# A two-layer transformer tower on one core: attention scores in row halves, and the value products one iteration later

## The reference, cut to what matters

```python
def _L0_attn_ref(x, Wq, Wk):              # x: a sequence's normed rows, 512 x 64
    q = jnp.einsum('bnd,ed->bne', x, Wq)
    k = jnp.einsum('bnd,ed->bne', x, Wk)
    attn = jax.nn.softmax(jnp.einsum('bid,bjd->bij', q, k) * scale, axis=-1)
    return jnp.einsum('bij,bjd->bid', attn, x)
def _L1_attn_ref(x, Wq, bq, Wk, bk, Wv, bv, Wo, bo):
    weights = jax.nn.softmax(jnp.einsum('bsd,btd->bst', q, k) * scaling, axis=-1)
    return jnp.einsum('bst,btd->bsd', weights, v) @ Wo.T + bo
```

## Time and profile before

| | |
|---|---|
| median of three runs | 935.1 us (934.78 to 936.87) |
| the profiled execution's own time, and its span | 936.95 us, 935.1 us |
| busy share of the span: PE, PEld, DVE, ACT, POOL | 95%, 68%, 65%, 62%, 41% |
| TensorE's mean granted clock | 0.991 |
| maximum reductions L743 | 256, 170.4 us busy, 687 ns each |
| value products L1058 (records) | 1024, 124.7 us busy |
| score products L1049, L1050, L1024 | 256 each; 113.1, 101.6, 108.2 us busy |
| exponentials L504 | 256, 146.0 us busy, 596 ns each |

### The profile page before, as it was taken

How to read it: one execution, slowest core, us unless ns; L and a number is a source line. 1 busy time by engine, 2 the same in 40 slices (tenths; PEclk the granted TensorE clock), 3 DMA queues, 4 the chain that set the end, 5 groups by cost and what they waited for, 6 DMA issues and landing times.

```text
span 935.1 us, 21847 instructions
## 1 busy us (share of the span) xinstructions
PE 891.6 (95%) x6198; PEld 631.5 (68%) x6198; DVE 603.8 (65%) x2610; ACT 576.6 (62%) x1195; POOL 384.1 (41%) x523
## 2 busy tenths in 40 slices
PE   4879999999999999979999999999999999999998
PEld 2657666666766676656666676666777777777775
DVE  5876777778787899967777777774434343434321
ACT  1336666666666666646666666666666666666664
POOL 0133444444437888834444344443333333333300
PEclk9999999999999999989999999999999999999999
DMA  4000000000001222200000000000000000000000
GB/s 103 2 1 2 1 0 0 0 0 0 1 1 49 72 73 68 75 7 1 1 0 0 0 0 1 1 1 7 12 18 11 17 11 17 11 17 11 18 13 23
DMA packets 18995, 15.13 MB, mean 16 GB/s; under 512 B 5762, under 2 KB 18946, under 8 KB 18946
## 3 DMA queue, kind: packets, MB, share of 16 engines
q1 hardware_dynamic: 18946, 14.52, 5.6%
HBM read 10.32 MB, written 4.19 MB: 16 GB/s over the span
## 4 chain that ended last, share of the span: by engine, by line
PE 83%; DVE 12%; issue 2%; ACT 1%; DMA 1%; DVEq 0%; POOL 0%; SPq 0%; ACTq 0%
PE bank L1226 13%; PE bank L1058 13%; PE bank L1206 7%; PE bank L1024 7%; PE bank L1207 6%; PE bank L971 5%; DVE nmax L743 5%; PE bank L1049 5%; PE bank L1050 5%; PE bank L1135 4%; PE bank L996 3%; PE bank L1037 2%; PE bank L1013 2%; PE bank L1014 2%; PE bank L1003 2%
## 5 line engine op out<-in xcount | busy, mean ns | idle before, releaser
L743 DVE TENSOR_REDUCE nmax<-bank 128x1 fp32r<-128x512 f32 x256 | 170.4, 687 | 47.7 <-PE bank L1024 47.5
L360 POOL TENSOR_TENSOR XS<-XN,XS 128x252 fp32r<-128x252 f32 x128 | 98.0, 765 | 211.6 <-ACT XS L402 211.6
L342 POOL TENSOR_TENSOR rstd<-VE,half 128x4 f32<-128x4 f32 x128 | 129.2, 1009 | 119.6 <-DVE VE L661 119.6
L504 ACT ACTIVATE PT<-bank 128x512 f32<-128x512 f32 x256 | 146.0, 596 | 41.8 <-PE bank L1050 35.5
L354 POOL TENSOR_TENSOR XN<-XC,rstd 128x252 f32<-128x252 f32 x128 | 78.3, 612 | 183.9 <-PE bank L1058 183.7
L556 ACT ACTIVATE PT<-bank 128x512 f32<-128x512 f32 x256 | 132.2, 605 | 3.5 <-PE bank L1207 2.8
L475 ACT ACTIVATE OT<-bank 128x256 f32<-128x256 f32 x96 | 36.8, 384 | 154.3 <-PE bank L1058 103.8
L1058 PE MATMUL bank<-PT,XN 128*64 128x256 f32 x1024 | 124.7, 386 | 0.0
L1226 PE MATMUL bank<-PT,W 128*64 128x256 f32 x1024 | 124.5, 386 | 0.0
L1024 PE MATMUL bank<-X,QH 128*128 128x512 f32 x256 | 108.2, 424 | 8.6 <-DVE nmax L743 1.7
L1049 PE MATMUL bank<-QH,X 128*128 128x512 f32 x256 | 113.1, 442 | 0.5 <-ACT Q L497 0.5
(11 more groups left out here) (136 smaller groups left out, 1506.4 us busy)
## 6 DMA issues: line engine op xcount, KB each, us to landing
WR<-experts SPq DMA_DIRECT2D x64, 129.0 KB, 2.0
out<-H SPq DMA_DIRECT2D x32, 128.0 KB, 1.7
W<-pack SPq DMA_DIRECT2D x5, 252.5 KB, 3.9
W<-pack SPq DMA_DIRECT2D x1, 251.5 KB, 5.1
W<-pack SPq DMA_DIRECT2D x1, 243.0 KB, 5.6
tk<-tokens SPq DMA_DIRECT2D x1, 64.0 KB, 4.4
route_sb<-route SPq DMA_DIRECT2D x1, 0.2 KB
```

The source lines that it names most:

```text
L342: pl.tensor_tensor(rstd[:, par, :], VE[:, par, :], half[:, :], ALU.pow).then_inc(sigma_done, 1)
L504: sc_.activation(PT[:, par, kt, :], bank[4 + kt % 2][:, :], ACT.Exp, scale=SCALE).then_inc(s.e_ready, 1)
L743: v.tensor_reduce(nmax[:, par, t:t + 1], bank[2 + t % 2][:, :], axis=AX, op=ALU.max, negate=True).then_inc(s.max_ready, 1)
```

## The change

It does four things, in both attention stages.

1. **Row halves.** A copy `XD` of the rounded part is put on partitions 64 to 127, beside `X2`'s own on 0 to 63. The score products for the maxima (`pair_for_max`) now use 64 rows each: tile t on the upper half of the rows, tile t+1 on the lower, one right after the other, into banks 2 and 3. The low part of the scores (`low_scores`) is made in the same way into banks 4 and 5. So the maxima no longer see the rest of the keys, and the product of the two rests leaves the scores. The high part (`high_scores`) stays at 128 rows.
2. **Order.** TensorE's body i is now: spread i; project i+1; low part of tiles 0 and 1; turn back i-2; high part of tiles 0 and 1; first pair of maxima of i+1; three of the four values of i-1; second pair of maxima; the fourth; low and high part of tiles 2 and 3; turn i+2.
3. **Another bank for the maxima.** `spread_max` writes bank 0 (row 64, with 65 columns of weights, of which 64 are zero) in place of bank 7. As the turned rows pass through bank 0 too, it waits for `x2_ready` of i+1, which now comes after both copies, `X2` and `XD`. The row goes into row 64 of `QH` in place of row 0 of `Q2`.
4. **ScalarE and VectorE** follow: ScalarE copies bank 6 between exponentials 1 and 2 and rounds after the copies to `X2` and `XD`; VectorE finishes i-2 first, then takes all four maxima of i+1, then its low part.

```diff
@@ -38,7 +38,7 @@
-CONSTS = 7
+CONSTS = 8
@@ -236,8 +236,9 @@
+        XD = sb("XD", [P, 2, SEQ], F32R)
-        nmax = sb("nmax", [P, 2, NT], F32R)
+        nmax = sb("nmax", [P, 2, NT, D + 1], F32R)
@@ -331,8 +332,9 @@
-            pl.memset(f32(XS[:, :, :, D:D + 1]), 0.0).then_inc(consts_set, 1)
+            pl.memset(f32(XS[:, :, :, D:D + 1]), 1.0).then_inc(consts_set, 1)
+            pl.memset(f32(nmax[:, :, :, :]), 0.0).then_inc(consts_set, 1)
@@ -450,7 +452,10 @@
-                sc_.activation(X2[:, par, :], bank[0][:, :], ACT.Copy).then_inc(s.x2_ready, 1)
+                ins = sc_.activation(X2[:, par, :], bank[0][:, :], ACT.Copy)
+                if s is a0 or s is a1:
+                    ins = sc_.activation(XD[D:P, par, :], bank[0][0:D, :], ACT.Copy)
+                ins.then_inc(s.x2_ready, 1)
@@ -490,11 +495,9 @@
                 def body(i, par, lane):
-                    if not known(i) or i >= 1:
-                        evac_o(s, before, bank[6], i - 1, 1 - par)
-                    sc_.activation(Q2[0:1, par, :], bank[7][0:1, :], ACT.Copy).then_inc(s.m_ready, 1)
+                    sc_.activation(QH[D:D + 1, par, :], bank[0][D:D + 1, :], ACT.Copy).then_inc(s.m_ready, 1)
@@ -503,9 +506,10 @@
-                        if kt == 1:
-                            high_on(s, before, after, layer * 2, i + 3, 1 - par, (lane + 3) % 4)
+                        if kt == 1 and (not known(i) or i >= 1):
+                            evac_o(s, before, bank[6], i - 1, 1 - par)
+                    high_on(s, before, after, layer * 2, i + 3, 1 - par, (lane + 3) % 4)
@@ -740,7 +744,7 @@
                 def maxima(i, par, tiles):
                     for t in tiles:
-                        v.tensor_reduce(nmax[:, par, t:t + 1], bank[2 + t % 2][:, :], axis=AX, op=ALU.max,
+                        v.tensor_reduce(nmax[:, par, t, D:D + 1], bank[2 + t % 2][:, :], axis=AX, op=ALU.max,
@@ -753,21 +757,20 @@
+                maxima(0, 0, range(NT))
                 low_parts(0, 0)
-                maxima(0, 0, range(NT))
                 def body(i, par):
+                    if not known(i) or i >= 2:
+                        finish(i - 2, par)
                     if has(i + 1):
+                        maxima(i + 1, 1 - par, range(NT))
                         low_parts(i + 1, 1 - par)
-                        maxima(i + 1, 1 - par, range(2))
-                    if not known(i) or i >= 1:
-                        finish(i - 1, 1 - par)
-                    if has(i + 1):
-                        maxima(i + 1, 1 - par, range(2, NT))
+                finish(NSEQ - 2, 0)
@@ -1013,41 +1016,45 @@
-                def scores_for_max(i, par, t):
+                def pair_for_max(i, par, t):
-                    if t >= 2:
-                        pe.wait_ge(s.max_ready, i * NT + (t - 1))
-                    elif not known(i) or i >= 1:
-                        pe.wait_ge(s.max_ready, i * NT + (t - 1))
-                    mm(bank[2 + t % 2][:, :], QH[:, par, t * P:(t + 1) * P], X2[:, par, :],
-                       start=True, stop=True).then_inc(s.s_ps, 1)
+                    if t == 2 or not known(i) or i >= 1:
+                        pe.wait_ge(s.max_ready, i * NT + t)
+                    for own, rows, keys in ((t, slice(0, D), X2), (t + 1, slice(D, P), XD)):
+                        mm(bank[2 + own % 2][:, :], QH[rows, par, own * P:(own + 1) * P], keys[rows, par, :],
+                           start=True, stop=True).then_inc(s.s_ps, 1)
                 def spread_max(i, par):
+                    if has(i + 1):
+                        pe.wait_ge(s.x2_ready, i + 2)
+                    else:
+                        pe.wait_ge(after.x2_ready, 1)
-                    if not known(i) or i >= 1:
-                        pe.wait_ge(s.m_ready, i)
-                    if not known(i) or i >= 2:
-                        pe.wait_ge(s.h_done, i - 1)
                     for t in range(NT):
-                        last = mm(bank[7][0:1, t * P:(t + 1) * P], nmax[:, par, t:t + 1],
+                        last = mm(bank[0][0:D + 1, t * P:(t + 1) * P], nmax[:, par, t, :],
-                def scores(i, par, kt):
-                    if kt == 0:
-                        pe.wait_ge(s.m_ready, i + 1)
-                    if kt >= 2 or not known(i) or i >= 1:
-                        pe.wait_ge(s.e_ready, i * NT + (kt - 1))
-                    cols = slice(kt * P, (kt + 1) * P)
-                    o = bank[4 + kt % 2][:, :]
-                    mm(o, X2[:, par, cols], QH[:, par, :], start=True, stop=False)
-                    mm(o, X2[:, par, cols], Q2[:, par, :], start=False, stop=True).then_inc(s.st_ps, 1)
+                def low_scores(i, par, kt):
+                    pe.wait_ge(s.ql_ready, i + 1)
+                    if kt == 2 or not known(i) or i >= 1:
+                        pe.wait_ge(s.e_ready, i * NT + kt)
+                    for own, rows, keys in ((kt, slice(0, D), X2), (kt + 1, slice(D, P), XD)):
+                        mm(bank[4 + own % 2][:, :], keys[rows, par, own * P:(own + 1) * P], Q2[rows, par, :],
+                           start=True, stop=False)
+                def high_scores(i, par, kt):
+                    pe.wait_ge(s.m_ready, i + 1)
+                    for own in (kt, kt + 1):
+                        mm(bank[4 + own % 2][:, :], X2[:, par, own * P:(own + 1) * P], QH[:, par, :],
+                           start=False, stop=True).then_inc(s.st_ps, 1)
@@ -1069,34 +1076,36 @@
-                for t in range(NT):
-                    scores_for_max(0, 0, t)
+                for t in (0, 2):
+                    pair_for_max(0, 0, t)
                 def body(i, par, lane):
                     spread_max(i, par)
                     if has(i + 1):
                         project(i + 1, 1 - par)
+                    low_scores(i, par, 0)
+                    if not known(i) or i >= 2:
+                        turn_back(s, before, i - 2, par)
+                    high_scores(i, par, 0)
+                    if has(i + 1):
+                        pair_for_max(i + 1, 1 - par, 0)
+                    if not known(i) or i >= 1:
+                        for kt in range(NT - 1):
+                            values(i - 1, 1 - par, (lane + 3) % 4, kt)
+                    if has(i + 1):
+                        pair_for_max(i + 1, 1 - par, 2)
+                    if not known(i) or i >= 1:
+                        values(i - 1, 1 - par, (lane + 3) % 4, NT - 1)
+                    low_scores(i, par, 2)
+                    high_scores(i, par, 2)
                     turn_on(s, after, i + 2, par)
-                    scores(i, par, 0)
-                    scores(i, par, 1)
-                    if has(i + 1):
-                        scores_for_max(i + 1, 1 - par, 0)
-                    if not known(i) or i >= 1:
-                        turn_back(s, before, i - 1, 1 - par)
-                    scores(i, par, 2)
-                    if has(i + 1):
-                        scores_for_max(i + 1, 1 - par, 1)
-                    scores(i, par, 3)
-                    if has(i + 1):
-                        scores_for_max(i + 1, 1 - par, 2)
-                        scores_for_max(i + 1, 1 - par, 3)
-                    if not has(i + 1):
-                        pe.wait_ge(s.ql_ready, NSEQ)
-                        meanwhile()
-                    for kt in range(NT):
-                        values(i, par, lane, kt)
+                turn_back(s, before, NSEQ - 2, 0)
+                pe.wait_ge(s.ql_ready, NSEQ)
+                meanwhile()
+                for kt in range(NT):
+                    values(NSEQ - 1, 1, (NSEQ - 1) % 4, kt)
@@ -1284,14 +1293,20 @@
     def wide(m):
+    def once(m):
+        m = wide(m)
+        m[:, D] = 0.0
+        return m
     def led(first, m):
-    put("wq0", wide(led(none, x["L0_attn_Wq"])))
+    put("wq0", once(led(none, x["L0_attn_Wq"])))
-    put("wq1", wide(led(x["L1_attn_bq"], x["L1_attn_Wq"])))
+    put("wq1", once(led(x["L1_attn_bq"], x["L1_attn_Wq"])))
@@ -1310,7 +1325,7 @@
-    put("ct", wide(ct))
+    put("ct", once(ct))
```

## The result

The change makes the kernel slower by a fifth: 1120.8 us in the profiled execution, against 935.9 us (median of four runs before); the ratio is 1.198, with a 95% interval of 1.195 to 1.201. Of four runs of the changed kernel two took 1120.8 and 1120.9 us; in the other two (1143 and 1150) the granted clock was lower still, 0.90 in place of 0.92 over the span, and the ratio leaves these out. Forecast were 1035 us and at most 1085: the direction held, the size did not.

What follows compares the result with a forecast made beforehand. The prediction took TensorE to bound the kernel (83% of the chain of waits). 60 intervals x 1.70 = 102 us, less 2, gave +100: span 935.1 to 1035, execution 1037, median forecast 1035 us; range 968 to 1085.

Steps and rivals of the forecast that it cites:

- The new wait: Before the spread into bank 0: TensorE idles some 1.7 us per iteration until `X2` and `XD` are copied.
- The switches: Around row-halved products on TensorE: 0.10 us per switch and 0.11 for first weights, as for column halves.
- The rival of cheap switches: At the row-halved couples: switches cost little, +0.60 us per iteration, 972 us in all; chance 0.18.
- that of halves that run apart: At the couples: halves don't run together, three couples add 0.69 us per iteration, 1076 us; chance 0.10.
- The walk: One attention iteration followed through TensorE, ScalarE and VectorE: from 6.77 to 8.47 us, +1.70; chance as walked 0.46.
- The clock: Rival: granted clock falls after the wait, slowing three value products every second iteration; 40 us more, 1075 us; chance 0.19.
- the sum: Over both attention stages: 60 intervals x 1.70 = 102 us, less 2 for shorter first bodies, +100.
- the long run of values in each iteration: Reason given against the clock falling: TensorE's value products in every iteration; three of them take 1.3 us.
- The range: Whole kernel: 968 to 1085 us, leaving out the faster rival and the meeting of two dear cases.
- the far end where two of the dear cases meet: Whole kernel: two of the slower cases holding at once, left outside the upper bound of 1085 us.
- The rival of a faster kernel: In attention: TensorE stays the bound, copies done by turn's end, maxima hidden; 828 to 925 us, say 880; chance 0.05.

Runs made afterwards that it cites:

- x3: The changed kernel with full 128-row products for the couples, no copy to `XD`, and five idle-time products after each iteration's turn: 1030.9 us.
- x1: The changed kernel with seven idle-time products, read by nobody, after the turn of each iteration: 1067.6 us.
- x6: The kernel before, with values one iteration later in one block, turn of i+2 ahead of them, full rows, maxima in bank 7: 924.0 us, ratio 0.987.
- x8: x6 with idle-time products in the waits at both attention stages' starts and at the ends of the routed stage and a1: 918.2 us, ratio 0.982.

## Why the prediction was wrong, point by point

- **The new wait: right in its place and size, not in all of its reason.** TensorE stands idle for 1.69 us before the spread (forecast: some 1.7), 60 such waits end with the copy to `XD`, and x3 shows that the copy sets the time one for one. But the prediction puts bank 0 first, and by the code the late turn is enough: `project(i + 1)`, right behind the spread, waits for `x2_ready` at i + 2 by itself, the same count. With the maxima in another bank only the spread (0.29 us) could have gone ahead of the wait. That is read from the code; no run has the late turn without bank 0.
- **The switches: right, and for rows too.** Project to low couple 0.33, couple to the next 0.43, a first high product of 0.50: the column-halved rows were the right ones. The rival of cheap switches (972 us) and that of halves that run apart are both refuted. The Trainium skill's page "TensorEngine Tiling (Array Packing)", section "Key Properties", with its drain at a change of mode, agrees with these rows. So does the Trainium skill's page "TensorE: Matmul & The Clock Gate", Part 3, on products of different row groups that start some 4 ns apart (186.79 both).
- **The walk: right in its steps, 0.38 short in its sum** (8.47 forecast, 8.85 measured). Four terms: `X2` to `XD` takes 0.62, not 0.49 (193.38 to 194.00); from the end of `XD` to the spread it is 0.14, not 0.05; the spread with 65 columns of weights holds 0.29, not 0.24; the finish takes 1.13, not 1.00 (187.97 to 189.10). Together 0.40. The last of them is a misread price: the 1.00 of the earlier trace rows is the finish of one iteration, and in 22 of 30 iterations of a0 before it took 1.11 to 1.13. Over 62 intervals the walk at full clock is 24 us dearer; x1, with its first intervals and stage ends, measures 131 us where 100 were forecast.
- **The clock: the step that failed.** In "How the numbers follow" it stood as a rival of the walk, with a chance of 0.19 and its own 40 us, and the sum put it at nothing. It is no rival: x1 shows that TensorE's idle time in the wait, the same wait that makes the walk long, is what brings the clock down; so both come together and add up, 53 us for the clock. The evidence was there, a stretch behind the turn that looked "much the same" as the one before an observed fall; it got a small weight because of "the long run of values in each iteration". That reason did not hold: the fall comes ahead of the values, on project, the low couple, the turn back and the high products (0.54 from 195.01), and the values run at full clock. The rival's 40 us came near by luck. It had 1.3 us in 31 iterations, on the values; measured are 1.33 us (10.11 - 8.78) in 37, on other products.
- **The range** left out "the far end where two of the dear cases meet". That is where the result lies: 1035 + 24 for the walk + 53 for the clock = 1112, above the upper bound of 1085. Of the 9 us that are still missing, 6 lie outside the 62 intervals, between the two attention stages and behind the second, where the clock before was 1.00 (625 to 658) and now is 0.90 (804 to 837).
- **The rival of a faster kernel** failed for the reason that was given against it: the copies stand behind exponentials 2 and 3. x6 shows that its idea was not empty: with the copies beside the values TensorE is the bound again, and the kernel is faster than before.

## What to carry to other kernels

When a producer moves behind the work that used to cover its latency, or a buffer is reused so that one engine waits for another, walk one iteration through all engines before counting what was saved on one of them. Four couples in place of eight full products, 0.92 us less work by count, were worth 0.09 on the chain, and the chain that the wait closes made the iteration 2 us longer. Price a half-array product with its way in and out; alone between full products it costs more than the two full products that it replaces. And ask of idle time on TensorE for two costs, the wait itself and a lower clock after it, and add them where both are at work: idle-time products in a wait tell them apart, and can even stay in.

## What the runs showed of the hardware

- Work added to a waiting TensorE made the kernel faster: 7 products per iteration, 1120.8 to 1067.6 us; in x8, 32 products in the whole kernel, 924.0 to 918.2 us.
- A copy from partitions 0 to 63 of PSUM to partitions 64 to 127 starts 0.62 us after the copy ahead of it from the same bank (193.38 to 194.00), where a rounding starts 0.48 after it (x3: 216.71 to 217.19). Why was not tried.
- Two row-halved products started within 0.01 us of each other in every iteration looked at, and their switches cost what those of column-halved ones do: 0.10 us on each side (186.46 to 186.79, 186.79 to 187.22) and 0.11 for the first weights (a record of 0.50 at 186.79, where a full product's is 0.39).
